# Counting edges by groups of three tiles in place of five, in a graph-network kernel on one core

## The reference

```python
edge_index = jnp.stack([src, dst])
x = _layernorm(x + _L0_gnn_ref(x, src, dst, ...), axis=-1)
x = _layernorm(x + _L1_gnn_ref(x, edge_index, ...), axis=-1)
return x
```

```python
e = jax.nn.leaky_relu(a1[src] + a2[dst], negative_slope=NEG_SLOPE)
w = jnp.exp(e - m[dst])
denom = jax.ops.segment_sum(w, dst, num_segments=n)
msg = (w / denom[dst])[:, :, None] * ft[src]
agg = jax.ops.segment_sum(msg, dst, num_segments=n)
```

## Time and profile before

| | us |
|---|---|
| median of 3 runs | 1123.72 |
| lowest, highest | 1122.53, 1124.12 |
| profiled execution | 1125.33 |
| its span | 1123.6 |
| busy in the span: PE, DVE, ACT, POOL | 1056.6, 952.6, 642.1, 143.4 |
| first one-hot tile to end of last addition | 11.5 to 79.7 |

### The profile page before, as it was taken

The page is one execution under the profiler, slowest core; times in us unless marked ns, Lnnn a source line. Parts: engine busy times, 40 slices in busy tenths (PEclk is TensorE's granted clock), DMA queues, the critical chain, the costliest instruction groups (busy, mean ns, idle before and its releaser), DMA issues.

```text
span 1123.6 us, 20575 instructions
## 1 busy us (share of the span) xinstructions
PE 1056.6 (94%) x8048; PEld 909.6 (81%) x8048; DVE 952.6 (85%) x1531; ACT 642.1 (57%) x939; POOL 143.4 (13%) x155
## 2 busy tenths in 40 slices
PE   6996899989898989999999999999999999999996
PEld 4665666666666667999999999999988888888885
DVE  7989999999999999986863999999987874397865
ACT  8658899999999898223111567666612311234331
POOL 1000000000000000000073112020400153411111
PEclk9998999999999999999999999999999999999998
DMA  4061020202020205533237310204041124343211
GB/s 150 1 227 52 3 92 1 93 1 92 2 92 1 98 1 177 175 116 120 76 109 266 126 47 1 84 1 151 20 169 57 43 95 173 131 160 127 77 61 53
DMA packets 40022, 98.99 MB, mean 88 GB/s; under 512 B 4505, under 2 KB 17393, under 8 KB 39925
## 3 DMA queue, kind: packets, MB, share of 16 engines
q1 hardware_dynamic: 39926, 97.66, 25.1%
HBM read 70.74 MB, written 26.90 MB: 87 GB/s over the span
## 4 chain that ended last, share of the span: by engine, by line
PE 62%; DVE 19%; ACT 10%; issue 7%; DMA 1%; DVEq 0%; POOL 0%; SPq 0%; POOLq 0%; ACTq 0%
PE psum L1110 14%; PE psum L1019 13%; PE psum L1071 12%; PE psum L1149 8%; DVE R L1692 8%; DVE R L1678 5%; ACT R L1288 5%; PE psum L1034 4%; ACT R L1304 3%; PE psum L759 3%; PE psum L944 1%; PE psum L1087 1%; PE psum L1140 1%; PE psum L1122 1%; PE psum L895 1%
## 5 line engine op out<-in xcount | busy, mean ns | idle before, releaser
L944 PE MATMUL psum<-ident,R 128*128 128x128 f32 (+3 forms) x1200 | 158.3, 281 | 37.0 <-ACT R L1288 36.6
L944 PEld LDWEIGHTS psum<-ident,R 128*128 128x128 f32 (+3 forms) x1200 | 128.9, 143 | 77.5 <-ACT R L1288 64.7
L1692 DVE CUSTOM_DVE_ANT_0 R<-R,LC 128x1250 f32<-128x1250 f32 x120 | 175.7, 1467 | 0.2 <-DVE LC L1664 0.2
L1288 ACT ACTIVATE R<-R,row_max 128x1250 f32<-128x1250 f32 x120 | 161.7, 1348 | 1.7 <-DVE row_max L1692 1.5
L958 PE MATMUL psum<-R 128*64 128x256 f32 (+3 forms) x1200 | 147.8, 385 | 0.6 <-ACT R L1304 0.6
L1304 ACT COPY R<-psum 128x1280 f32<-128x1280 f32 x120 | 143.7, 1198 | 1.5 <-PE psum L944 1.5
L1019 PE MATMUL psum<-w_hi,x1T_hi 128*128 128x256 f32 (+1 forms) x480 | 127.0, 283 | 0.0
L1019 PE MATMUL psum<-w_hi,x1T_lo 128*128 128x256 f32 (+1 forms) x480 | 125.7, 280 | 0.9 <-DVE x1T_lo L1784 0.9
L1019 PE MATMUL psum<-w_lo,x1T_hi 128*128 128x256 f32 (+1 forms) x480 | 123.9, 280 | 0.0
L1678 DVE SCALAR_TENSOR_TENSOR R<-R 128x1250 f32<-128x1250 f32 x80 | 122.3, 1530 | 0.0
L2179 POOL TENSOR_TENSOR rstd<-rstd,minus_half 128x1 f32<-128x1 f32 (+1 forms) x40 | 33.8, 845 | 664.5 <-DVE rstd L1707 664.5
(11 more groups left out here) (234 smaller groups left out, 2489.6 us busy)
## 6 DMA issues: line engine op xcount, KB each, us to landing
R<-rows_spill SPq DMA_DIRECT2D x20, 625.0 KB, 5.2
rowbuf<-rows_spill SPq DMA_DIRECT2D x14, 625.0 KB, 5.1
lc_spill<-LC SPq DMA_DIRECT2D x9, 625.0 KB
LC<-lc_spill SPq DMA_DIRECT2D x9, 625.0 KB, 5.3
res_spill<-colbuf SPq DMA_DIRECT2D x36, 128.0 KB, 2.9
R<-res_spill SPq DMA_DIRECT2D x9, 512.0 KB, 3.5
R<-in_x_dram SPq DMA_DIRECT2D x1, 3456.0 KB
res_spill<-R SPq DMA_DIRECT2D x9, 384.0 KB
```

The source lines that it names most:

```text
L944: last = e.transpose(turn0[r % 2][0:m, s, 0:n_dst], ring[0:n_dst, r % RING0, s * P:s * P + m], ident[0:n_dst, 0:n_dst])
L1288: e.activation(ring[0:m, r % RING0, :], ring[0:m, r % RING0, :], ACT.Exp, bias=row_max[0:m, r % RING:r % RING + 1], scale=-1.0, accum_out= ...
L1692: e.tensor_tensor_reduce(slot, slot, LC[0:m, i, :], -1.0, MIN_CEILING, ALU.add, ALU.min, row_max[0:m, r % RING:r % RING + 1]).then_inc(S.l ...
```

## The change

Groups have three tiles in place of five (57 groups, the last with two), windows 32 destinations in place of 48, so `hot_cell` has 320 columns and a window matmul is 128 x 320. Sums take turns in three banks (0, 4, 1); an addition stands three groups behind, and PE waits for the addition three groups back. The segments go: a whole group is now the unit of the order, with 7 groups ahead of the x turns, three more per four turns, 22 ahead of the projections and three more (nine tiles) per two projections. The turned rows have bank 5 alone, one piece each after projections 11, 12 and 13. The ring of ten `hot_cell` and the `hot_row` tables for ten tiles stay. As 57 x 3 isn't 170, `groups_i` is loaded by two DMAs (the last group's row holds the last 375 edges), and the arithmetic by group has a second instruction for the last group.

```diff
--- before.py
+++ after.py
...
         return range(c // P, (c + w + P - 1) // P)
 
     RING = 8
-    GT = 5
-    GROUPS = ET // GT
-    WIN = 48
+    GT = 3
+    GROUPS = (ET + GT - 1) // GT
+    WIN = 32
     KEPT = GROUPS - 1
     HT = NT // 2
-    assert GROUPS * GT == ET and GROUPS % 2 == 0 and NT % 2 == 0 and NT * WIN <= BANK
+    assert KEPT * GT < ET and NT % 2 == 0 and NT * WIN <= BANK
 
     x1_dram = nc.dram_tensor("x1_spill", (N, D), F32, kind="Internal").ap()
     base_dram = nc.dram_tensor("base_spill", (N, D), F32, kind="Internal").ap()
...
             assert edge_at[0] <= RING * N
             return ap
 
-        HOT = 2 * GT
+        HOT = 10
         edge_rows = [(0, P), (P, ET - P)]
         iota_h = edge_view([N], F16)
         PROJ, KG, XW = C0 + 2, KT // 2, 2 * P
         RHS_AT = NT * D + 4 * P
-        hot_at = [RHS_AT + KT * PROJ + j * (NT * WIN // 2) for j in range(GT + 1)]
-        assert hot_at[GT] <= NT * (D + XW)
-        hot_cell = [edge_view([NT * WIN], BF16, EP) for _ in range(GT)]
-        hot_cell += [view(R2, at, [NT * WIN], BF16, EP) for at in hot_at[0:GT]]
-        PAIR = 2 * GT
+        hot_at = [RHS_AT + KT * PROJ + j * (NT * WIN // 2) for j in range(HOT // 2 + 1)]
+        assert hot_at[HOT // 2] <= NT * (D + XW)
+        hot_cell = [edge_view([NT * WIN], BF16, EP) for _ in range(HOT // 2)]
+        hot_cell += [view(R2, at, [NT * WIN], BF16, EP) for at in hot_at[0:HOT // 2]]
+        PAIR = HOT
         hot_rows = [edge_view([P, PAIR], BF16, EP) for _ in range(2)]
         iota_rows = edge_view([P, PAIR], F16, EP)
         assert PAIR % 2 == 0 and ET % PAIR == 0
...
         edges_i = [edge_view([EP], I32) for _ in range(4)]
         edges_f = [edge_view([EP]) for _ in range(4)]
         groups_i = edge_view([GT * EP], I32, GROUPS)
-        assert iota_at <= 4 * N and edge_at[0] >= 6 * N
+        edge_at[0] = max(edge_at[0], 6 * N)
+        assert iota_at <= 4 * N
         hot_full = [edge_view([N], BF16, EP) for _ in range(2)]
         hot_part = [edge_view([2 * P], BF16, EP) for _ in range(2)]
         src_f, dst_f = (edge_view([ET], F32, EP) for _ in range(2))
...
             return (banks[7], banks[3], banks[6], banks[2])[turn % 4]
 
         def row_bank(n):
-            return banks[7] if n >= NP else banks[5] if n % 2 else banks[1]
+            return banks[7] if n >= NP else banks[5]
 
         def proj_psum(c):
             return psum[:, 6:8, 0:KG * PROJ] if c % 2 else psum[:, 2:4, 0:KG * PROJ]
...
                 at += rows[i]
             return places
 
-        def window_psum(half):
-            return banks[4 * half][:, 0:NT * WIN].rearrange("p (i w) -> p i w", w=WIN)
+        WIN_BANKS = [banks[0], banks[4], banks[1]]
+        AHEAD = len(WIN_BANKS)
+
+        def window_psum(g):
+            return WIN_BANKS[g % AHEAD][:, 0:NT * WIN].rearrange("p (i w) -> p i w", w=WIN)
 
         all_sum = [[banks[0], banks[1], banks[2]], [banks[4], banks[5], banks[6]]]
         PREP_EDGES_F, PREP_MAX, PREP_CLIP, PREP_ENDS = 4, 6, 7, 8
-        PREP_SRC, PREP_PARTS, PREP_BASE_I, PREP_BEHIND, PREP_WIDEST, PREP_BASE, PREP_REL, PREP_CELL = 9, 11, 13, 14, 15, 17, 18, 19
+        PREP_SRC, PREP_PARTS, PREP_BASE_I, PREP_BEHIND, PREP_WIDEST, PREP_BASE, PREP_REL, PREP_CELL = 9, 11, 13, 14, 15, 17, 19, 20
 
 
         def sync_program(e):
-            e.dma_start(groups_i, dst.rearrange("(g e) -> g e", g=GROUPS)).then_inc(S.groups_in, 16)
+            e.dma_start(groups_i[0:KEPT, :], dst[0:KEPT * GT * EP].rearrange("(g e) -> g e", g=KEPT)).then_inc(S.groups_in, 16)
+            e.dma_start(groups_i[KEPT:GROUPS, :], dst[E - GT * EP:E].rearrange("(g e) -> g e", g=1)).then_inc(S.groups_in, 16)
             for k, ids in enumerate((dst, src)):
                 for r, (t0, n) in enumerate(edge_rows):
                     e.dma_start(edges_i[2 * k + r][0:n, :], ids[t0 * EP:(t0 + n) * EP].rearrange(
...
                 e.wait_ge(S.y_out[b], 16 * (len(range(b, NT, 4)) + (b == i % 4)))
 
 
-        def windows_pe(e, g, tiles):
-            if g >= 2 and tiles[0] == 0:
-                e.wait_ge(S.win_added, g - 1)
-            for j in tiles:
-                e.wait_ge(S.win_hot, g * GT + j + 1)
-                hot_row = hot_rows[g // 2 % 2][:, :, g % 2 * GT + j]
-                e.matmul(banks[4 * (g % 2)][:, 0:NT * WIN], hot_row, hot_cell[(g * GT + j) % HOT], start=(j == 0),
-                         stop=(j == GT - 1)).then_inc(S.win_free, 1)
+        def group_tiles(g):
+            return range(g * GT, min(g * GT + GT, ET))
+
+        def windows_pe(e, g):
+            if g >= AHEAD:
+                e.wait_ge(S.win_added, g - AHEAD + 1)
+            tiles = group_tiles(g)
+            for t in tiles:
+                e.wait_ge(S.win_hot, t + 1)
+                hot_row = hot_rows[t // PAIR % 2][:, :, t % PAIR]
+                e.matmul(WIN_BANKS[g % AHEAD][:, 0:NT * WIN], hot_row, hot_cell[t % HOT], start=(t == tiles[0]),
+                         stop=(t == tiles[-1])).then_inc(S.win_free, 1)
 
         def all_pe(e):
             def product(buf, g, start, stop):
...
                         product(buf, g, False, False).then_inc(S.all_free, 1)
                 product(None, g, False, True).then_inc(S.all_sum, 1)
 
-        SEGMENTS = [range(0, 3), range(3, GT)]
-        COUNTS = len(SEGMENTS) * GROUPS
-        W_COUNTS, FIRST_COUNTS, TURN_COUNTS = 2, 8, 26
+        W_COUNTS, FIRST_COUNTS, TURN_COUNTS, STEP = 2, 7, 22, 3
 
         def x_counts(turn):
-            return FIRST_COUNTS + turn // 4 * 2 * len(SEGMENTS)
+            return FIRST_COUNTS + turn // 4 * STEP
 
         def proj_counts(pair):
-            return TURN_COUNTS + pair // (2 * KG) * 2 * len(SEGMENTS)
-
-        assert x_counts(KT * NP - 1) < TURN_COUNTS and proj_counts(NT * KT - 1) <= COUNTS - 2 * len(SEGMENTS)
-        row_turns = {NT + 1: range(NP - 1), NT + 3: range(NP - 1, NP)}
+            return TURN_COUNTS + pair // (2 * KG) * STEP
+
+        assert x_counts(KT * NP - 1) < TURN_COUNTS and proj_counts(NT * KT - 1) <= GROUPS - 2
+        row_turns = {NT + 1 + n: range(n, n + 1) for n in range(NP)}
 
 
         def pe_program(e):
...
             span = e.value_load(base_i[0:1, GROUPS:GROUPS + 1], min_val=0, max_val=N)
             e.sem_inc(S.all_free, 2)
 
-            def count_segment(n):
-                g, part = divmod(n, len(SEGMENTS))
+            def count_group(g):
                 with e.If(span < WIN):
-                    windows_pe(e, g, SEGMENTS[part])
-                if n == 0:
+                    windows_pe(e, g)
+                if g == 0:
                     with e.Else():
-                        for bank in (banks[0], banks[4]):
+                        for bank in WIN_BANKS:
                             last = e.matmul(bank[:, 0:NT * WIN], zeros[:, 0:P], zeros[:, 0:NT * WIN], start=True, stop=True)
                         last.then_inc(S.win_free, ET)
-                if n == COUNTS - 1:
+                if g == GROUPS - 1:
                     with e.Else():
                         all_pe(e)
 
             def count_until(done, n):
                 for at in range(done, n):
-                    count_segment(at)
+                    count_group(at)
                 return max(done, n)
 
             done = count_until(0, W_COUNTS)
...
                 c, w = pieces[piece]
                 if piece == 0:
                     e.wait_ge(S.ft, NT * (g + 1))
-                if n >= 2:
-                    e.wait_ge(S.rowsT, 2 * (n if n >= NP else n - 1))
+                if n >= 1:
+                    e.wait_ge(S.rowsT, 2 * n)
                 for i in tiles_of(piece):
                     m = rows[i]
                     last = e.transpose(row_bank(n)[0:HG, i * P - c:i * P - c + m], att[0:m, i, g * HG:(g + 1) * HG],
...
                 last.then_inc(S.ft_sum, 1)
                 for n in row_turns[c] if c in row_turns else ():
                     turn_rows(n)
-            count_until(done, COUNTS)
+            count_until(done, GROUPS)
 
 
             e.wait_ge(S.counted, 1)
...
                     e.wait_ge(S.cleared, 3)
                 else:
                     e.wait_ge(S.win_kept, g)
-                e.copy(CT[:, :, bass.ds(base + 1, WIN - 1)], window_psum(g % 2)[:, :, 1:WIN]).then_inc(S.win_kept, 1)
+                e.copy(CT[:, :, bass.ds(base + 1, WIN - 1)], window_psum(g)[:, :, 1:WIN]).then_inc(S.win_kept, 1)
 
             def keep_until(kept, counts):
-                for g in range(kept, min(counts // len(SEGMENTS), KEPT)):
+                for g in range(kept, min(counts, KEPT)):
                     keep_window(g)
-                return max(kept, min(counts // len(SEGMENTS), KEPT))
+                return max(kept, min(counts, KEPT))
 
             kept = keep_until(0, W_COUNTS)
             bank = side_bank(0)
...
                     "p s (k h) -> p s k h", h=2), sums[:, :, :, C0:PROJ].rearrange("p k h s -> p s k h")).then_inc(S.ft, 1)
```

(47 more changed lines are left out.)

## The result

The changed kernel takes 1131.46 us in the median of six runs (1130.92 to 1131.87); the kernel before, in six runs taken beside it, 1123.92. That is 7.5 us slower, where 8.0 us faster was forecast. One of the six took 2648.3 us; the median of the other five is 1123.72. The ratio is 1.0077, 95% interval 1.0067 to 1.0087. It is estimated from all runs of both kernels and isn't the quotient of the two medians (1.0067); either way the loss is clear of the noise. The median is also, within 0.1 us, the time that rival 3 named.

What follows compares the result with a forecast made beforehand. DVE bounds the counting beside the x turns, PE beside the projections, waits the tail. Counting ends at 71.7 in place of 79.7: 8.0 us off 1125.33 gives 1117.3, and 1.6 to the median gives 1115.7 us; range 1111.5 to 1121.2.

Steps and rivals of the forecast that it cites:

- rival 3: Counting on DVE: register loads after additions come to light, 0.58 us each at every second place, total 1131.4 us; chance 0.05.
- Prices on DVE: One-hot tiles on DVE: 0.214 us each in place of 0.254, 6.8 us less in all; narrow additions 0.08 us.
- Additions go from 34 to 57 ... plus one register load each, priced below: DVE's additions in the counting: 23 more narrow ones at 0.08 us, 1.8 us more, plus one register load each.
- I cost it at nothing: ACT's group copies, 56 in place of 33: at most 12.8 us more, covered by 13.6 us free; cost nothing.
- Prices on PE: Window matmuls on PE: 0.16 us each, between 0.138 and 0.207; nine tiles and two projections take 3.2 us.
- rival 1: Counting: DVE alone is the bound, PE blocks 2.84 us, counting ends at 68.3, total 1112.3 us; chance 0.20.
- Start: Before the first tile: one more DMA, +0.41 us, and one more subtraction, +0.08; first tile at 11.96, not 11.47.
- Beside the x turns: DVE's tiles 23 to 65: 13.3 us, so the projections start at about 34.4 in place of 36.9.
- Beside the projections: First two projections 1.49 us, nine blocks of 3.2, 0.5 for row turns; end at 65.2 in place of 73.7.
- Tail: End of the counting: 4.6 us of remaining DVE work, then 1.9 for last sums; ends at 71.7 us.
- Rival 4: PE's granted clock falls beside the projections, up to 2.84 us more per block, 1127 at four; chance 0.03 with Rival 5.
- Rival 5: A group spans all 32 destinations and the general path runs, over 700 us slower; 1 in 100.

Runs made afterwards that it cites:

- e1: Changed kernel with the base loaded on DVE once in place of 57 times, counts left incomplete: 1121.07 us, ratio 0.9986 to the kernel before.
- e2: Changed kernel with the base loaded only once on DVE and once on ACT, counts left wrong: 1113.87 us, ratio 0.9919 to the kernel before.
- e4: Changed kernel with the ten stores of the residual issued behind the last addition: 1127.11 us, ratio 1.0033 to the kernel before.
- e12: Changed kernel without range checks on DVE and ACT, residual stores moved behind the counting: 1117.43 us, ratio 0.9958 to the kernel before.
- e8: Changed kernel with groups set back to five tiles over 48 destinations, three banks kept: 1121.32 us, ratio 0.9987 to the kernel before.
- e5: Changed kernel with four bases per register load on DVE and ACT, range checks kept: 1144.51 us, ratio 1.0188 to the kernel before.

## Why the prediction was wrong

- *Prices on DVE.* The tile: ten take 2.21 us from 11.20 on, (2.21 - 0.30) / 9 = 0.212 us; 0.214 was forecast. The narrow addition at 0.08 us holds where no load shows. Right.
- *"Additions go from 34 to 57 ... plus one register load each, priced below".* This is the step that failed. Below, in rival 3, a load got a price only where an addition has to wait, and the forecast's sum has none at all. A load has a price each time: 0.51 us of DVE's sequencer, whether an addition waits or not. With three tiles, an addition and a load, groups came 0.97 us apart where the sequencer set the pace, and the engine needs 0.71. Even with its share of the row table (3/10 of 0.74) the engine needs 0.93, and the lead that a row table gives lasted for one group.
- *ACT: "I cost it at nothing."* The second step that failed. I compared the time of ACT's copies with its idle time; its 23 further loads, 0.45 us each on its sequencer, aren't busy time either. They were worth 7.4 us of counting with DVE's gone (e1 to e2). And I looked at the third stretch alone; more than half of the 7.4, 3.9 us, lies ahead of the projections.
- *Prices on PE.* A matmul cost 0.137 us, the lower end of 0.138 to 0.207, against my 0.16. With no loads the counting ends at 70.7, where the forecast had 71.7 and rival 1 68.3. So the sum was right, to 1.0 us, for a kernel whose loads are free. In part its terms offset each other: the projections began at 35.4 in place of 34.4, and the last two of them at 62.9 in place of 63.7.
- *Start.* The first tile came at 11.20, not 11.96 (before 11.47). Which of the terms was off no run separates.
- *Beside the x turns.* 18.4 us (21.3 to 39.7) against 13.7; the terms listed there give 13.3, and 20.6 and 13.3 make 33.9, not the 34.4 that the sum went on with. ACT's loads are most of what was missing. *Beside the projections* nine blocks took 32.9 us with the row turns, 3.66 each, against 3.2 and 0.5. *Tail:* 13.0 against 6.5, of which 3.5 by the residual's stores (e4).
- *Rival 3* named the register load and a total of 1131.4 us, and the median was 1131.46; but its mechanism was half right. It wanted additions that wait for ACT's copy, at every second place. Gaps came mostly without such waits, behind 42 of the loop's 54 additions, and most of them of 0.25 us in place of 0.58. The total agrees by luck. Its argument against, that a sum is ready long before its addition, was true and beside the point.
- *Rival 4.* The granted clock was 1.00 up to 78 us and 0.50 from there on, behind the last projections, so no block suffered. By the rule of the Trainium skill cited there ("TensorE: Matmul & The Clock Gate", part 1) the transposes behind the tail run at half rate in both kernels, as they did; e12 shows the 1.8 us that this costs. But in e8 and e12 PE had such gaps too, of 2.73 and 1.39 us, and its clock stayed at 1.00, so a gap alone doesn't bring the half rate.
- *Rival 5* didn't come up. Its 700 us weren't worked out from rows, and no run shows them.

That the residual's stores lengthen the loads I had not in the sum at all, though the tail before has a gap of 0.86 us that I left without a reason; its two loads there took 0.93 us each.

## What to carry to other kernels

In this kernel each engine had two times: what it is busy, and what its sequencer needs to feed it. Before cutting work into smaller pieces, look up in the view of single source lines what each piece costs the sequencer (register loads, range checks, address arithmetic), multiply by the new number of pieces, and compare that with the engine's time per piece, for every engine that follows the pieces. If it is more, leave out checks that the data already satisfy, keep large stores out of SBUF away from stretches with register loads, and don't gather the loads in one place.

## What the runs showed of the hardware

- A register load from SBUF with one word took 0.30 us on DVE's sequencer and 0.28 on ACT's; with four words 0.96 and 0.91. Beside the stores of the residual (DMA share 1.03, 414 GB/s, 77 to 84 us of the changed kernel) it took 0.89 to 1.36 us on DVE, and with four words up to 3.2 on DVE and 3.9 on ACT (e5). With the DMA engines as full of rows loaded into SBUF (1.01, 418 GB/s, e12) it took 0.31.
- The range check behind it is two sequencer instructions, 0.183 and 0.023 us on DVE, 0.152 and 0.018 on ACT.
- VectorE's groups, 0.71 us of work each, came 0.97 us apart with a load and its check in each (changed kernel, 43.11 to 44.08), and 0.71 apart for one group behind a row table.
- A matmul of 128 x 320 followed the one before by 0.137 us at the granted clock of 1.00 (e2), with another weight load for each.
- A gap of 2.73 us in PE's work left the granted clock at 1.00 (e8), and it fell to 0.50 just behind one of 1.33 (the kernel before, 80 us).
